# A graph layer on one core: two of every seven edge chunks summed on TensorE, and the sort placed behind the first layer in some steps

## What is computed

```python
h = relu(layernorm(x))
xw = h @ W_in
W_ij = (shifted_softplus(edge_attr_20 @ W_f1 + b_f1) @ W_f2 + b_f2) * edge_weight1
x_ij = xw[dst] * W_ij                       # one row of 128 per edge
out = segment_sum(x_ij, src, 6250)          # rows of the same src are added up
x + shifted_softplus(out @ W_o1 + b_o1) @ W_o2 + b_o2
```

## Time and profile before

| | us |
|---|---|
| median of 3 runs | 2346.69 (2345.57 to 2347.01) |
| the profiled execution, its own time | 2347.22 |
| its span | 2345.4 |
| PE busy | 2170.7 (93%) |
| PE weight load busy (beside PE) | 1364.1 (58%) |
| DVE busy | 1848.2 (79%) |
| ACT busy | 1788.5 (76%) |
| POOL busy | 1850.0 (79%) |

### The profile page before, as it was taken

One profiled execution on the slowest core, in us unless ns is written; L12 is line 12 of the kernel. 1 busy time (PEld: TensorE's weight loads), 2 busy tenths in 40 slices (PEclk: granted clock), 3 DMA queues, 4 the chain that ended last, 5 costly groups with the idle time before them and its releaser, 6 DMA issues.

```text
span 2345.4 us, 56553 instructions
## 1 busy us (share of the span) xinstructions
PE 2170.7 (93%) x16953; PEld 1364.1 (58%) x16953; DVE 1848.2 (79%) x3897; ACT 1788.5 (76%) x4171; POOL 1850.0 (79%) x1182
## 2 busy tenths in 40 slices
PE   7599999999999999999999999999999999999945
PEld 4466566666656656666666666656666665666613
DVE  5678788878888888888878887887888878887758
ACT  4588888888888788888878888888888888788803
POOL 1488888888888888888888888888888888888852
PEclk9799999999999999999999999999999999999968
DMA  9465655666565666666556666566565666666564
GB/s 356 125 98 91 92 91 90 91 92 91 89 91 92 89 92 90 92 89 93 89 90 92 90 91 91 91 90 91 91 91 89 91 91 90 92 90 90 78 181 167
DMA packets 350174, 239.83 MB, mean 102 GB/s; under 512 B 89295, under 2 KB 337551, under 8 KB 349539
## 3 DMA queue, kind: packets, MB, share of 16 engines
q0 software_dynamic: 164000, 77.47, 34.6%
q1 hardware_dynamic: 184651, 158.26, 25.2%
q10 hardware_dynamic: 1212, 0.42, 0.1%
HBM read 139.86 MB, written 96.12 MB: 101 GB/s over the span
## 4 chain that ended last, share of the span: by engine, by line
PE 35%; DMA 32%; POOL 13%; issue 13%; DVE 3%; ACT 3%; POOLq 0%; ACTq 0%; SPq 0%; DVEq 0%
DMA acc<-region,target 30%; POOL acc L598 13%; PE ps L1308 10%; PE ps L1327 8%; PE ps L1287 6%; PE ps L1294 4%; PE ps L1274 2%; PE ps L1363 2%; PE ps L1282 2%; ACT region L741 1%; DMA w_f<-in_L_gnn_W_f_dram 1%; PE ps L1241 0%; ACT region L765 0%; DVE region L1153 0%; POOL parts L591 0%
## 5 line engine op out<-in xcount | busy, mean ns | idle before, releaser
L598 POOL DMA_INDIRECT acc<-region,target x1132 | 1802.9, 1593 | 361.5 <-issue 256.4
L1308 PE MATMUL ps<-region 128*128 128x386 bf16 x3024 | 650.5, 336 | 67.1 <-ACT region L741 65.7
L741 ACT ACTIVATE region<-ps 128x386 bf16<-128x386 f32 x756 | 372.6, 493 | 209.8 <-PE ps L1308 202.5
L1327 PE MATMUL ps<-region 64*128 64x448 bf16 x4536 | 497.4, 352 | 9.5 <-DVE region L1036 9.5
L1308 PEld LDWEIGHTS ps<-region 128*128 128x128 bf16 x3024 | 253.5, 97 | 368.0 <-issue 138.2
L997 DVE SCALAR_TENSOR_TENSOR region<-ps,bf_negative,region 128x512 f32<-128x512 f32 x391 | 292.7, 749 | 190.3 <-ACT region L727 185.2
L765 ACT ACTIVATE region<-ps,cut_col 128x128 f32<-128x128 f32 x1564 | 440.3, 363 | 0.7 <-PE ps L1363 0.7
L1287 PE MATMUL ps<-w_f,region 128*128 128x128 f32 x3128 | 438.6, 284 | 0.0
L1287 PEld LDWEIGHTS ps<-w_f,region 128*128 128x128 f32 x3128 | 384.3, 194 | 0.0
L723 ACT ACTIVATE region<-ps,bf 128x512 f32<-128x512 f32 x391 | 268.9, 688 | 74.9 <-PE ps L1274 72.2
L1294 PEld LDWEIGHTS ps<-region 128*128 128x128 f32 x2264 | 294.1, 191 | 27.5 <-DVE region L997 6.2
(11 more groups left out here) (133 smaller groups left out, 1630.8 us busy)
## 6 DMA issues: line engine op xcount, KB each, us to landing
dst_b<-dst_rows SPq DMA_DIRECT2D x391, 128.0 KB
src_b<-src_rows SPq DMA_DIRECT2D x283, 128.0 KB
acc<-region,target POOLq DMA_INDIRECT x1132
attrT<-in_edge_attr_dram SPq DMA_DIRECT2D x782, 20.0 KB
acc<-region SPq DMA_DIRECT2D x20, 640.0 KB, 18.6
xwin<-xw_parts SPq DMA_DIRECT2D x391, 31.5 KB
region<-acc SPq DMA_DIRECT2D x48, 256.0 KB, 4.9
xw_parts<-parts SPq DMA_DIRECT2D x12, 384.0 KB, 2.3
```

The lines of the kernel that those rows point to most:

```text
L598: nc.gpsimd.indirect_dma_start(out=acc[a], out_offset=bass.IndirectOffsetOnAxis(ap=target[:, slot, t:t + 1], axis=0), in_=summed[:, slot, ...
L741: nc.scalar.activation(binned[:, h, j, :], binned_ps[:, 0:PC], ACT.Copy).then_inc(s_binned, 1)
L1308: ins = MM(binned_ps[:, 0:PC], place[:, h % 2, t, j * P:(j + 1) * P], payload_high[:, h % 2, t, :], start=(t == 0), stop=(t == T - 1))
L1327: ins = MM(ps[6 + r][:, 0:NL], binned[rows, slot, j, part * F:(part + 1) * F], in_node[rows, sums_until(kk, i) % 2, slot, :], start=(d == ...
```

## The change

Two of every seven chunks go to PE: chunk c when c % 7 is 2 or 5, for the first 110 (the last one is chunk 383). By the same planner every turn is then filled from step 5 to the early turn of step 390, each step of the steady part has a job of node sums, and after step 392 there are seven jobs (steps 393 to 399). There are 281 POOL chunks. The ranks are counted for 108 chunks as before, and for the two left over in one more set of ten small matmuls, one multiplication and one reduction (`spare_ranks`). On PE the early sort of step k keeps its place when chunk k-2 is a POOL chunk; when chunk k-2 is a PE chunk (a step without same-source sums) it moves behind `hidden_product`, that is behind `filter_bias` of chunk k and the first layer of chunk k+1. The orders of ACT, DVE, SP and POOL are not changed.

```diff
-U = 25
-ON_PE = (2, 6, 9, 13, 16, 20, 24)
-NPE = 108
+U = 7
+ON_PE = (2, 5)
+NPE = 110
+BANK_QCS = 36
...
-    BANK_QCS = NPE // 3
+    MAIN = 3 * BANK_QCS
+    SPARE = NPE - MAIN
...
-                link(V.tensor_tensor(ps_all[:, 4:7, 0:n], ps_all[:, 4:7, 0:n], in_bin[:, t, :, :].rearrange("p (s n) b -> p s (n b)", s=3), ALU.mult))
-                V.tensor_reduce(rank[:, t, :].rearrange("p (s n) -> p s n", s=3), ps_all[:, 4:7, 0:n].rearrange("p s (n b) -> p s n b", b=BINS),
+                link(V.tensor_tensor(ps_all[:, 4:7, 0:n], ps_all[:, 4:7, 0:n], in_bin[:, t, 0:MAIN, :].rearrange("p (s n) b -> p s (n b)", s=3), ALU.mult))
+                V.tensor_reduce(rank[:, t, 0:MAIN].rearrange("p (s n) -> p s n", s=3), ps_all[:, 4:7, 0:n].rearrange("p s (n b) -> p s n b", b=BINS),
                                 AX.X, ALU.add).then_inc(s_rank, 1)

+            def spare_ranks():
+
+                counts = ps[3][:, 0:T * SPARE * BINS].rearrange("p (t m) -> p t m", t=T)
+                dve.wait_ge(s_rkps, T + 1)
+                link(V.tensor_tensor(counts, counts, in_bin[:, :, MAIN:NPE, :].rearrange("p t n b -> p t (n b)"), ALU.mult))
+                V.tensor_reduce(rank[:, :, MAIN:NPE], counts.rearrange("p t (n b) -> p t n b", b=BINS), AX.X, ALU.add).then_inc(s_rank, 1)
+
             def most():
-                dve.wait_ge(s_rank, T)
+                dve.wait_ge(s_rank, T + 1)
...
+            def spare_ranks():
+
+                w = SPARE * BINS
+                for t in range(T):
+                    for b in range(t + 1):
+                        ins = MM(ps[3][:, t * w:(t + 1) * w], ones_bf[:, :] if b < t else later_bf[:, :],
+                                 in_bin[:, b, MAIN:NPE, :].rearrange("p n b -> p (n b)"), start=(b == 0), stop=(b == t))
+                ins.then_inc(s_rkps, 1)
...
             ranks(T - 1)
+            spare_ranks()
             pe.wait_ge(s_rmax, 1)
...
             def hybrid_products():
+                def sort_early(jobs):
+                    for kk, h, i, late in jobs:
+                        if not late:
+                            bin_up(kk, h, i)
+
...
                     jobs = sorts_at.get(k, ())
-                    for kk, h, i, late in jobs:
-                        if not late:
-                            bin_up(kk, h, i)
+                    if pool_chunk(k - 2):
+                        sort_early(jobs)
                     n = k
                     if exists(n):
                         after(pe, s_msg, n - 1)
                         filter_bias()
                     n = k + 1
                     if exists(n) and n > 0:
                         after_slot(pe, s_attr, n, 2)
                         after(pe, s_h, n - 1)
                         wait(pe, s_last_sum, pool_until(n - 3))
                         hidden_product(n % 4)
+                    if not pool_chunk(k - 2):
+                        sort_early(jobs)
```

More of the change, by code:

```diff
@@ L43, in gnn_kernel @@
     PC = 3 * F + 2
-    BANK_QCS = NPE // 3
+    MAIN = 3 * BANK_QCS
+    SPARE = NPE - MAIN
     assert all((n >> 6) * SEVENTH >> 11 == n // NL for n in range(N))
-    assert N == BINS * NL and NL % 64 == 0 and NL <= 512 and NPE == 3 * BANK_QCS and BANK_QCS * BINS <= 512
+    assert N == BINS * NL and NL % 64 == 0 and NL <= 512 and BANK_QCS * BINS <= 512 and 0 < SPARE and T * SPARE * BINS <= 512
     assert JT == 2 * SLOTS - 1
```

## The result

| | before | after |
|---|---|---|
| median, us | 2346.85 (2345.57 to 2349.32, 4 runs) | 2367.53 (2365.89 to 2367.75, 4 runs) |
| ratio, 95% interval | | 1.0087 (1.0075 to 1.0099) |
| the profiled execution, its own time | 2347.22 | 2365.89 |
| its span | 2345.4 | 2363.5 |

What follows compares the result with a forecast made beforehand. PE and POOL were taken as level within 0.5%, PE setting the pace after the change; 2347.22 + 8 (loop's end) + 0.3 (before the loop) = 2355.5 for the profiled execution, median forecast 2355.0, range 2343 to 2367.

Steps and rivals of the forecast that it cites:

- The stall changes its name: PE's loop stall moves from the early sort behind ACT to `filter_bias` behind DVE's message, some 110 times at 0.55 us.
- The pace: Seven steady steps take 38.55 us on PE, their five POOL chunks need 37.95, so PE sets the pace.
- The refilled turns and node sums (+5.7): PE's loop: filling empty sort turns costs 2.5 us and steps without node sums 3.5; two shorter steps give back 0.3.
- the order's +5.5: PE's loop: the moved early sort costs 0.05 us for each of 110 PE chunks; range 0 to 22 us.
- L1282 of a late chunk is 11.2 us later: `filter_bias` late in the loop starts later by the sum 5.5 + 2.5 + 3.5 - 0.3.
- the +0.3 for the spare ranks: Before the loop: DVE's `spare_ranks` operations add 0.6 us, fewer copies save 0.35; sum +0.3, range 0 to 1.
- 2271.3 + 0.1 + 3.3 = 2274.7: Loop's end: the last scatter waits for one held by the reload and lands at 2274.7, 8.8 us later than before.
- any scatter that is in flight when the reload starts lands behind it: Loop's end: rule applied to the scatter four before the last, expected to start 0.5 us ahead of the reload.
- The first ("POOL is the bound", 2331.5): Rival for the loop: the new place fills PE's stall, so POOL bounds the kernel at 2331.5 us; chance 0.14.
- The later softplus: Rival on ACT: the late sort's copy holds up the next early sort by 0.2 us, 2371.5 in all; chance 0.13.
- The refilled turns and the order are free: Rival for PE's loop: only the node sums cost, 3.2 us on PE, giving 2349 us; chance 0.16.
- The last: Rival on POOL: DVE work of more PE chunks slows scatters, mean above 1.62 us, time 2380 us; chance 0.02.

Runs made afterwards that it cites:

- e4: The changed kernel, but in steps without same-source sums PE does the next chunk's first layer first, then the early sort, then `filter_bias`; 2345.27 us, ratio 0.9987.
- e2: The changed kernel with the old order of the early sort (two of seven chunks, 110 in all); 2354.90 us, ratio 1.0021.
- e1: The kernel before with the new order of the early sort alone (7 of 25 chunks, 108 in all); 2361.27 us, ratio 1.0068.
- e5: The changed kernel with the old order of the early sort in steps below 30; 2360.04 us, ratio 1.0058.
- e9: The kernel of e4, unchanged, run on a third chip; 2329.50 us, ratio 0.9926.
- e11: The kernel of e4 with its last DVE wait written twice, without a wait for scatters, on the third chip; 2330.45 us, ratio 0.9923.
- e3: The changed kernel, but DVE waits for all scatters before its long addition of 6.69 us; 2363.09 us, ratio 1.0066.
- e6: The kernel of e4 plus the wait of e3, DVE waiting for all scatters before its long addition; 2323.80 us, ratio 0.9901.
- e7: The kernel before (7 of 25 chunks, 108 in all) with the same edit as e4; 2338.28 us, ratio 0.9965.
- e8: The kernel of e4 with the reload of `x` behind the first four groups' accumulator loads and the addition just before its use; 2326.43 us, ratio 0.9911.
- e10: The kernel of e6, unchanged, run on the third chip; 2326.61 us, ratio 0.9916.

## Why the prediction was half right

**The stall changes its name: right.** 110 x 0.55 was expected for L1302 behind L1099, and 100 x 0.64 came in the steady stretch. e4 is the counter-test: where `filter_bias` isn't the first piece either, the wait goes.

**The pace: right.** 38.55 for seven steps was forecast and measured. The refilled turns and node sums (+5.7) came at +5.3 by e2; the order's +5.5 is 6.8 by the difference of the two kernels behind chunk 12 (12.1 against 5.3). It is 0.06 per PE chunk, near the 0.05 that was taken. Some 0.02 to 0.03 of it is the later PE that the prediction saw. The rest isn't what it weighed (an ACT copy not covered): at one of the two places of the seven-step pattern 19 of 49 steps take 4.76 to 4.84 instead of 4.63, as the message itself is later, and it is DVE that is late. Two such steps, of chunk 69 (4.78) and of chunk 41 (4.63):

```profile
474.62 0.51 DVE L998 TENSOR_SCALAR moved<-region,weight_limit,spare_row 128x4 f32<-128x4 f32 x1
...
478.45 0.67 DVE L1099 TENSOR_TENSOR region<-ps,region 128x512 f32<-128x512 f32 x1
```

```profile
320.65 0.28 DVE L998 TENSOR_SCALAR moved<-region,weight_limit,spare_row 128x4 f32<-128x4 f32 x1
...
324.31 0.69 DVE L1099 TENSOR_TENSOR region<-ps,region 128x512 f32<-128x512 f32 x1 [0.23 <-issue]
```

In the fast step DVE stands idle for 0.23 ahead of the message; in the slow one its small L998 takes 0.51 and no idle time is left. In each of the 19 steps L998 took 0.51 to 0.61, and in each a scatter of POOL had started 0.30 ahead of `filter_bias`; in 29 of the other 30 it took 0.28 or 0.29. Why it takes longer there isn't shown. With 7 in 25 the same order costs 12.1 behind chunk 12 (e1), because it takes the savings of the empty turns with it: 6.8 and 5.3 are the two parts of that.

**"L1282 of a late chunk is 11.2 us later": the first failed step.** The sum counted steady steps only, and took all at the start as it was. The first twelve steps lost 6.6, of which the new order has 4.9 (e2 and e5, with the old one, lose 1.7 there; e1, the new order with the old split, loses 3.0). The row was read for its 0.05 of latency; it also said that in the first steps `filter_bias` already waits for its message. There a wait moved onto the message grows from 1.56 to 2.0 and 2.3, and behind each of these PE's granted clock was 0.50, 1.2 GHz, for 6.8 and 3.4 us (that the length of the wait alone brings this about is refuted by e1 and e6). In return the prologue was no dearer: the first `filter_bias` lies 1.9 earlier, but over the experiments that start varies between -3.9 and +1.3 with no relation to the edit, so the +0.3 for the spare ranks can't be told.

**"2271.3 + 0.1 + 3.3 = 2274.7": the second failed step.** That the fourth scatter before the last is held by the reload, and that the last waits for it, came true, in part by luck. The rule was "any scatter that is in flight when the reload starts lands behind it", for a scatter 0.5 ahead of the reload. This one started 0.51 behind it, and the one that was in flight, started at 2263.23, landed at 2270.2 by its semaphore, 6 us ahead of the reload. The last scatter started 5.7 later than worked out: 5.0 are the late landing, nearly all of it the start's loss carried along, and 0.7 lie between landing and start, 0.77 where 0.1 had been put. Then the 3.3 of a usual landing was taken for a scatter that starts 0.1 behind the landing of the reload, and that is when DVE's addition begins, by the trace of before: L1134 at 2265.63, right behind the reload's landing, for 6.69. Before, no scatter was left to lie beside it. The 3.3 became 8.85. The prediction held such stretching to be small, on the scatters of the loop (at most 2.22 us), where DVE's pieces are about 1 us long; the one operation six times as long, right at the place that the change moves scatters into, wasn't asked. In the changed kernel, e2, e4, e5, e9 and e11 a scatter that met the addition took 7.17 to 7.20, and in the kernel before, e1, e3, e6, e7, e8 and e10, where none met it, the longest took 2.22 to 2.28. The Trainium skill, "SBUF — State Buffer", section "SBUF: two separate sides", says that a DMA issued by GpSimd can't write its descriptors while VectorE holds the ports that both share; of VectorE operations with two SBUF inputs, as this addition, it says that they hold them only against GpSimd operations that read SBUF. The runs show that such an addition does hold a scatter, for what is left of it; whether the scatter counts as an operation that reads SBUF, they don't tell.

**The sum again**, from the forecast's 2355.5 for the profiled execution: +5.3 for the loop (16.8 instead of 11.2 + 0.3), +5.6 for the stretched scatter, +0.8 that I had rounded away (8 for 8.8), -1.9 for what lies behind the last landing (77.6 instead of 79.5 to the span's end, for which no cause is shown). That is 2365.3, and 2365.9 was measured.

**The rivals.** The first ("POOL is the bound", 2331.5) fell for this kernel. Once `filter_bias` was moved too, POOL was the bound, at 2323.8 to 2330.5 on two chips and 2345.3 on a third. The later softplus didn't hold up the sorts: they wait 0.4 us in all. "The refilled turns and the order are free" is refuted by e1 and e2. The last had the right mechanism in the wrong place: in the loop the mean scatter stayed below its sign of 1.62, with 1.606.

## What to carry to other kernels

A reordering fills a stall only if what is now first in the queue is ready earlier than what stood there; here both were ready within 0.03 us of each other, and the piece that needs neither (the next chunk's first layer) was one place further down. Cost the first steps of a pipeline and its end by themselves, with what will lie side by side there after the shift, since a long VectorE operation may be harmless only because no GpSimd-issued transfer has been left to meet it. Compare kernels that hang on transfers on one chip only.

## What the runs showed of the hardware

One VectorE addition of two fp32 tiles in SBUF (128x6272, 6.69 us) stretched an indirect scatter issued by GpSimd from 1.55 us to between 7.17 and 7.20, in each of the six profiled executions (of five kernels) in which the two met; each time the scatter started 0.91 to 0.93 us into the addition. A load of 3.1 MB on SP's queue kept the scatters around its start from landing until it had landed: one that started 0.61 ahead of it in the kernel before landed 12.23 after its start, one 0.51 behind it in the changed kernel 11.23 after, where 3.3 is usual; one that started 1.34 ahead in the changed kernel landed 6 us before the reload did. PE's granted clock fell to 0.50 for 6.8 and 3.4 us right behind waits of 2.0 and 2.3 us in the changed kernel, and not behind waits of 1.6 us in e5; yet it stayed at full speed behind 2.0 us in e1 and fell behind 1.6 us in e6. And one and the same kernel, bound by scatters, took 2345.3 on one chip (ten runs) and 2329.5 on another (four), while the kernel before differed by 2.5 us; the cause is open.
